# Row sums of a windowed attention block: half of them from exponentials with an accumulator on ScalarE

## The reference

```
q, k, v = xn Wq' + bq, xn Wk' + bk, xn Wv' + bv      16 heads of 32
scores  = q k' / sqrt(32), masked where (i % 256) < (j % 256)
probs   = softmax(scores);  attn = probs v
s       = attn Wo' + bo
y       = clip((xn sign(Wf)') * scale + bias, -100, 100)
out     = x + s * y * sigmoid(y)
```

## Time and profile before

| | us |
|---|---|
| median of three runs | 1762.6 |
| profiled execution, device time | 1763.97 |
| its span, first to last instruction | 1762.2 |
| PE busy | 1701.8 |
| DVE busy | 1385.3 |
| POOL busy | 1295.9 |
| ACT busy | 972.8 |

### The profile page before, as it was taken

One profiled execution on the slowest core, in us unless ns is written; L12 is line 12 of the kernel. 1 busy time (PEld: TensorE's weight loads), 2 busy tenths in 40 slices (PEclk: granted clock), 3 DMA queues, 4 the chain that ended last, 5 costly groups with the idle time before them and its releaser, 6 DMA issues.

```text
span 1762.2 us, 33805 instructions
## 1 busy us (share of the span) xinstructions
PE 1701.8 (97%) x11996; PEld 792.9 (45%) x11996; DVE 1385.3 (79%) x2392; ACT 972.8 (55%) x1765; POOL 1295.9 (74%) x1280
## 2 busy tenths in 40 slices
PE   7998999999999999999999999999999999999888
PEld 3443444444444444444444444444444444444333
DVE  6888778797788877798778977778778797688862
ACT  4366655565555655556555566546665565555553
POOL 0087677886878778887788867798777886877883
PEclk9999999999999999999999999999999999999999
DMA  7313311242123412233122431224312232122111
GB/s 207 107 38 85 77 40 55 79 103 73 40 60 90 115 39 54 66 98 85 43 67 61 106 78 32 77 67 102 69 43 59 79 93 59 31 63 72 43 49 49
DMA packets 161273, 125.52 MB, mean 71 GB/s; under 512 B 83152, under 2 KB 135504, under 8 KB 160656
## 3 DMA queue, kind: packets, MB, share of 16 engines
q1 hardware_dynamic: 160144, 122.58, 26.6%
q10 hardware_dynamic: 960, 0.79, 0.2%
HBM read 41.23 MB, written 16.78 MB: 33 GB/s over the span
## 4 chain that ended last, share of the span: by engine, by line
PE 77%; DVE 9%; POOL 6%; issue 4%; ACT 3%; ACTq 0%; DMA 0%; SPq 0%; POOLq 0%; DVEq 0%
PE pJ L453 28%; PE pO L656 13%; PE pS L612 9%; PE pT L636 9%; POOL acc L1087 3%; PE pJ L545 3%; PE pJ L549 3%; PE pJ L546 3%; DVE mx L963 3%; PE pT L632 3%; PE pS L615 3%; PE pT L596 3%; DVE HL L934 2%; ACT PT L776 1%; ACT xs L693 1%
## 5 line engine op out<-in xcount | busy, mean ns | idle before, releaser
L1087 POOL TENSOR_TENSOR acc<-acc,PT 128x384 f32<-128x384 f32 (+1 forms) x744 | 884.2, 1222 | 280.1 <-PE pO L656 280.1
L963 DVE TENSOR_REDUCE mx<-pS 128x1 f32<-128x512 f32 (+3 forms) x1216 | 768.0, 649 | 193.1 <-PE pS L615 128.4
L776 ACT ACTIVATE PT<-pT 128x512 f32<-128x512 f32 (+1 forms) x960 | 537.0, 567 | 551.8 <-PE pT L636 496.1
L612 PE MATMUL pS<-QK 96*128 96x512 f16 (+3 forms) x1280 | 393.5, 318 | 20.9 <-DVE mx L963 19.9
L636 PE MATMUL pT<-QK 97*128 97x512 f16 (+3 forms) x1280 | 391.7, 317 | 6.4 <-DVE R L1006 3.9
L656 PE MATMUL pO<-PT,V 128*32 128x512 f32 (+3 forms) x2560 | 234.2, 473 | 0.2 <-ACT PT L776 0.2
L612 PEld LDWEIGHTS pS<-QK 96*128 96x128 f16 x1280 | 124.2, 97 | 195.4 <-DVE mx L963 58.5
L776 ACT ACTIVATE acc<-pT 128x512 f32<-128x512 f32 x256 | 151.4, 596 | 84.4 <-PE pT L636 82.0
L453 PE MATMUL pJ<-xT,wh_q 128*128 128x512 f16 x512 | 193.4, 380 | 1.9 <-ACT xT L711 1.5
L453 PE MATMUL pJ<-wh_v,xT 128*128 128x512 f16 x512 | 192.7, 379 | 1.6 <-DVE sg L952 1.6
L453 PE MATMUL pJ<-xT,wh_k 128*128 128x512 f16 x512 | 192.9, 378 | 0.0
(11 more groups left out here) (151 smaller groups left out, 2229.2 us busy)
## 6 DMA issues: line engine op xcount, KB each, us to landing
QK<-sg SPq DMA_DIRECT2D x756, 64.0 KB
xs<-in_x SPq DMA_DIRECT2D x60, 256.0 KB, 3.1
xr<-in_x SPq DMA_DIRECT2D x58, 256.0 KB, 3.0
out<-xr SPq DMA_DIRECT2D x58, 256.0 KB, 2.5
QK<-aT SPq DMA_DIRECT2D x256, 1.0 KB, 1.7
QK<-in_x SPq DMA_DIRECT2D x8, 256.0 KB, 3.7
QK<-in_mqk SPq DMA_DIRECT2D x2, 512.0 KB, 8.9
PT<-in_wvT SPq DMA_DIRECT2D x1, 1024.0 KB, 12.0
```

Source lines behind the costliest of these rows:

```text
L612: ins = e.matmul(s_bank("s", i)[:, base:base + wide], q4[0:96, j, qc], k4[0:96, j, 0:wide], start=True, stop=True)
L776: e.activation(to, t_bank("t", i)[:, 0:cols], ACT.Exp, scale=SS).then_inc(s_p, 1)
L963: e.tensor_reduce(mx[:, par, part, :].rearrange("p (j q) -> p j q", q=4)[:, heads[0]:heads[-1] + 1, qi], s_bank("s", i)[:, 0:cols].rearran ...
L1087: e.tensor_tensor(a, a, PT[:, RING_AT[i] % NPT, 0:width * len(heads)].rearrange("p (j q) -> p j q", j=len(heads)), ALU.add).then_inc(s_ap, 1)
```

## The change

For the 32 even units and for unit 63 (`ROW`, 33 units) the row sums come from the S chunks: once DVE has a chunk's maxima, it scales them at once to that chunk's shifts (`row_shifts`, L1023 of the new kernel), and ACT takes the exponential of the scores in place in PSUM, one instruction per head and query block, with the shift as its bias and a sum over the row written by the accumulator output (`sum_rows`, L808). A pS bank of such a chunk is free only after ACT has done so. For unit 63, whose rows lie in two chunks with two different maxima, the two partial sums are rescaled by exp of the differences and added. The 16 sums per row block are then moved by SP through a scratch in HBM into the layout that the reciprocals need (`move_sums`: one DMA, then four that wait for it). The even units have no additions on POOL and DVE any more, no product with ones and no first transpose; unit 63 has no products with ones, and unit 62 neither. The 31 odd units up to 61 are summed as before, with one acc instead of two. The ring has twelve rooms, and key block 0 of the even units goes through it too. For unit 63 DVE multiplies pO by the reciprocals directly and in two halves, and DVE instead of POOL makes the low halves.

The S chunks of an even unit are planned 1.4 units of time apart, those of an odd unit 0.82 apart, and nearly all other planned times change a little.

```diff
-NPT = 9
+NPT = 12
...
+                CHUNKS.append((38 * (_n // 2 - 1) + ((3 + 1.4 * _k) if _n % 2 == 0 else (18.3 + 0.82 * _k)),
+                               (_n, _qi, _part, _w, range(_j, _j + _heads))))
...
+ROW = [n for n in range(NU) if n % NQS == 0 or n == NU - 1]
...
 def at_sums(n):
-    return (at_pv(n + 1, 1) if n not in SUMMED else at_pv(n, 4 * (n % NQS) + 3)) + 0.01
+    return at_pv(n + 1, 1) + 0.01 if n not in ROW_AT else at_pv(n, 4 * (n % NQS) + 3) - -1.17
...
-        return SL * (a - 2) + ((3.97, 13.7, 17.61, 18.35), ...
+        return SL * (a - 2) + ((4.3, 15.37, 17.61, 18.51), ...
...
-        acc = sb("acc", [P, 2, 4, 512], F32)
+        acc = sb("acc", [P, 4, 512], F32)
...
+            if old == "s" and j in CHUNK_AT:
+                return s_e, CHUNK_AT[j] + 1
...
             def row_sums():
-                for n in range(NU - 2):
+                for n in range(NU):
+                    if n in ROW_AT:
+                        continue
...
-                        if n in SUMMED:
-                            if kb == 0:
-                                ln.wait_ge(*s_bank_free("sm", n))
-                            for j in range(4):
...
-                                ins = e.matmul(sums_bank(n)[32 * j:32 * j + 32, 512 - width:512], ones[:, :], probs,
-                                               start=kb == 0, stop=kb == nkb - 1)
...
+            def sum_rows():
+                for i in ROW_CHUNKS:
+                    n, qi, part, width, heads = S_TILES[i]
+                    yield at_s(i) + 1.81
+                    if ROW_AT[n] >= 2:
+                        ln.wait_ge(s_rq[ROW_AT[n] % 2], 64 * (ROW_AT[n] // 2))
+                    ln.wait_ge(s_ac, CHUNK_AT[i] + 1)
+                    for k, j in enumerate(heads):
+                        c = 4 * j + qi
+                        scores = s_bank("s", i)[:, k * width:k * width + width]
+                        ins = e.activation(scores, scores, ACT.Exp, bias=row_shift(i)[:, c:c + 1], scale=SS,
+                                           accum_out=rS[:, ROW_AT[n] % 2, part, c:c + 1])
+                    ins.then_inc(s_e, 1)
...
+            def row_shifts():
+                for i in ROW_CHUNKS:
...
+                    yield at_s(i) + 0.16 + 0.43
...
+                    ln.wait_ge(s_a, i + 1)
+                    of = (slice(None), slice(heads[0], heads[-1] + 1), qi)
+                    e.tensor_scalar(row_shift(i).rearrange("p (j q) -> p j q", q=4)[of],
+                                    mx[:, n % 2, part, :].rearrange("p (j q) -> p j q", q=4)[of], -SS, None,
+                                    ALU.mult).then_inc(s_ac, 1)
...
             def normalise():
...
+                    if n in ROW_AT:
+                        ln.wait_ge(s_rq[ROW_AT[n] % 2], 64 * (ROW_AT[n] // 2 + 1))
+                        e.reciprocal(rc[:, :], rq[:, ROW_AT[n] % 2].rearrange("p i q -> p q i")).then_inc(s_rc, 1)
...
+            def last_outputs():
+                for h in range(2):
...
+                    e.tensor_tensor(On[1][:, cs], pO[:, cs], R[:, cs], ALU.mult).then_inc(s_on, 1)
+                for h in range(2):
...
+                    e.tensor_tensor(last_half(Onl, h), On[1][:, 256 * h:256 * h + 256], last_half(Onh, h),
+                                    ALU.subtract).then_inc(s_ol, 1)
...
+            def move_sums():
...
+                    ln.wait_ge(s_e, chunks(n))
...
+                    e.dma_start(moved[par], rS[:, par, 0, :]).then_inc(s_rd[par], 16)
...
+                    ln.wait_ge(s_rd[par], 16 * (ROW_AT[n] // 2 + 1))
+                    for j in range(4):
+                        e.dma_start(rq[32 * j:32 * j + 32, par, :, :],
+                                    moved[par].rearrange("(i b) (j q) -> j b i q", b=32, j=4)[j]).then_inc(s_rq[par], 16)
```

More of the change, by code:

```diff
@@ L100, in at_s @@
 def at_s(i):
[L101 to L102 removed]
+    return CHUNKS[i][0]
 def at_t(i):
@@ L398, in gate, with last_half, row_shift, probabilities_at @@
             return xs[:, k, :] if 0 <= k < 4 else xr[k - 4][:, :] if k in (4, 5) else U[i % 2][:, :]
-        def sums_bank(n):
-            return s_bank("sm", n) if n in SUMMED else t_bank("sm", n)
+        def last_half(to, h):
+            return to[:, (GN - 1) % NSLOT, 512 + 256 * h:768 + 256 * h]
+        def row_shift(i):
+            n, _, part, _, _ = S_TILES[i]
+            return ap[:, part, :] if n == NU - 1 else a16[:, n % 2, 0:16]
+        def probabilities_at(i):
+            n, kb, width, heads = T_TILES[i]
+            if kb == 0 and n not in ROW_AT:
+                return acc[:, heads[0], :]
+            return PT[:, RING_AT[i] % NPT, 0:width * len(heads)]
         def bank(kind, a, b=0):
@@ L775, in probabilities @@
[L775 to L776 removed]
+                    if i not in RING_AT:
+                        ln.wait_ge(s_sm, n // 2)
+                    elif RING_AT[i] >= NPT:
+                        i0 = RING[RING_AT[i] - NPT]
+                        n0, kb0, _, _ = T_TILES[i0]
+                        ln.wait_ge(s_pv, units(n0) + kb0 + 1)
+                        if i0 in ADD_P_AT:
+                            ln.wait_ge(s_ap, ADD_P_AT[i0] + 1)
+                        elif i0 in ADD_V_AT:
+                            ln.wait_ge(s_av, ADD_V_AT[i0] + 1)
@@ L1038, in last_results @@
                     e.tensor_tensor(result(i), gate(i), rest(i), ALU.add).then_inc(s_fv, 1)
-            in_time(maxima(), shifts(), additions(), normalise(), constants(), split_weights(), output_bias(),
-                    first_layer_norm(), layer_norm(), split_x(), take_xt(), stage_qk(), gates(), results(), last_results())
+            in_time(maxima(), row_shifts(), shifts(), additions(), normalise(), constants(), split_weights(), output_bias(),
+                    first_layer_norm(), layer_norm(), split_x(), take_xt(), stage_qk(), gates(), last_outputs(), results(), last_results())
         @block.gpsimd
@@ L1090, in normalise @@
             def normalise():
-                for n in range(NU):
+                for n in range(NU - 1):
                     gn, qs = divmod(n, NQS)
                     s, cs = gn % NSLOT, slice(qs * 512, qs * 512 + 512)
-                    yield past("sm", n) + 1.01
+                    yield past("sm", n) + (0.32 if n in ROW_AT else 0.98)
                     ln.wait_ge(s_R, n + 1)
```

251 lines of the change are left out of this document (144 added, 107 removed).

## The result

The new kernel takes 1749.51 us (median of four runs, 1748.9 to 1751.11) against 1762.4 on the same chip: ratio 0.9929, interval 0.9912 to 0.9946. It is faster, by 12.9 us where 28.6 were forecast. A second measurement of it, later and beside its own runs of the kernel before (1762.99), gave 1749.88 and 0.9920 (0.9907 to 0.9934). The time is inside the range and almost exactly that of the accumulator case (1750), in part by luck, as shown further down. The profiled execution has a span of 1748.0, 14.2 less than before.

The account below looks back on a forecast made before the run. PE was taken to bound a batch; from a span of 1762.2 us, -26.7 - 7.7 - 0.5 + 7 + 3 + 5 - 5 - 4 = -28.9, plus 1.8 minus 1.4, gave 1734 us; range 1717 to 1757.

Parts of the forecast that it names:

- accumulator case: Rival, chance 0.20: each accumulator sum costs ACT 0.14 us extra, layer norm stretches cost 23 us instead of 7; 1750 us.
- PE's terms: On PE, 31 removed sums of even units save 26.7 us; removed products with ones of units 62 and 63 save 7.7.
- the end: After the last product with V, PE's other matmuls cover the shorter chain, so it gains only about 0.5 us.
- ring: Twelve rooms and faster additions mostly remove ACT's waits for POOL in the middle: 5 us gained (0 to 8).
- POOL: Near the end, where POOL is busy while PE idles, lighter POOL work gains 4 us (0 to 8).
- the forecast's own sign of being wrong: Forecast is wrong if PE's waits for pS and pT together exceed 60 us, or PE's work did not fall some 34.
- Score exponentials on ACT: On ACT, even units' exponentials (512 columns: 686 ns) add 6.5 us per unit; layer norm stretches overrun 1.1 us, seven batches.
- The accumulator: On ACT, writing the accumulator costs near nothing (upper bound 4.5 us per even unit); ACT's term 7 us, 0 to 39.
- Chain through DVE: In even units, late DVE scalings hold ACT's exponentials and make PE wait: 0.1 us per unit, 3 us in all.
- slower rival: Rival, chance 0.11: late DVE scalings hold T exponentials 2.2 us per even unit, 70 us; 1798 or more, as pauses lower clock.
- Unit 63: In the 30 us from 1660, 27 scalings and 32 exponentials fill DVE and ACT: 5 us lost (0 to 12).
- case of more gained: Rival, chance 0.15: half of PE's 27 us behind the maxima goes, ACT and unit 63 cost nothing; 1719 us.

Follow-up runs that it names:

- e2: New kernel with a single one-column exponential per score chunk in place of all its exponentials and sums: 1716.74 us, ratio 0.9731 to the kernel before.
- e1: New kernel with its score exponentials but without their accumulator output, sums taken from a constant: 1732.05 us, ratio 0.9816 to the kernel before.
- e10: New kernel with each scaling of a score chunk's maxima planned 0.01 instead of 0.43 units of time after the maxima: 1753.88 us, ratio 0.9933.
- e3: New kernel with unit 63 summed as before by products with ones, all else unchanged: 1745.38 us, ratio 0.9889 to the kernel before.
- e5: New kernel with nine rooms for probabilities instead of twelve: 1760.40 us, ratio 0.9973 to the kernel before.
- second trace: The new kernel run once more, unchanged, on the chip of the later experiments: 1749.88 us, ratio 0.9920 to the kernel before.
- e9: New kernel with unit 63 summed by products with ones and the second halves' f16 copies of x on POOL: 1737.09 us, ratio 0.9847.
- e4: New kernel with one more one-column ACTIVATE ahead of each of the 544 exponentials, nothing left out: 1806.70 us, ratio 1.0238 to the kernel before.

## Why the prediction was right or wrong

- **What bounds the kernel** (PE, and a matmul removed in the middle is worth its length): right. With most of ACT's new load gone (e2) 46.5 us of span come off; PE's terms, the end, ring and POOL were -26.7 - 7.7 - 0.5 - 5 - 4 = -43.9. The page of e2 shows the two halves: PE is busy for 33.8 us less than before, the forecast's 34, and idle for 12.7 less.

```profile
PE 1668.0 (97%) x11652; PEld 781.1 (46%) x11652; DVE 1319.9 (77%) x2621; ACT 1026.0 (60%) x2145; POOL 1158.1 (68%) x1154
```

  In the new kernel PE's busy time fell by only 19.6 us, so the forecast's own sign of being wrong, that PE's work did not fall by some 34 us, is there on the page. The matmuls are gone as planned; the other 14.2 us are time that PE takes longer over the same matmuls than in e2, where only ACT's load differs. Some 5 us of them are the clock, by my estimate from 0.992 of 1748.0 us granted against 0.995 of 1715.7; the rest no run separates.
- **Score exponentials on ACT**: right. By start-to-start times the forecast's 686 less 120 ns is 0.57 us for 512 columns, and 0.57 was measured; 581 less 120 is 0.46, and 0.46 was measured. For all that was budgeted against the gain (7 + 3 + 5 = 15 us) the exponentials without reads cost at least 13.5 (e1 against e2): 6 in the middle, where 7 + 3 were forecast, 5.3 at unit 63 and 2.3 at the start, which the sum left out.
- **The accumulator**: this is the step that failed. "What writing the accumulator costs, no row shows ... I take a value near nothing, because the accumulator belongs to an instruction that passes over the data anyway". It is an instruction of its own, 0.1 us of the stream, and the 544 of them cost 18.8 us (e1), more than the 14.7 by which the forecast missed; the other terms erred by 4 the other way. The formula would have borne it in part: with 0.1 us each the excess is 1.1 + 16 x 0.1 = 2.7 us, seven times, 19 us for the term in place of 7, so 11 us for the reads. They cost 11.9 in the middle, but only some 60% of what a batch lost lies in the layer norm group, where the formula put all, and 6.6 us lie at the start and at unit 63, outside it. The reason given was an argument about what the instruction does, not a row; the Trainium skill's rule for VectorE (VectorE: DVE Perf Modes, section on two Vector instructions with no wait between them), weighed beside it, pointed the other way.
- **The accumulator case** had the right mechanism: 0.14 us each, batch 211, 1750; measured 0.10, 210.3, 1749.5. That the time came out to half a microsecond is luck. With the 0.10 that was measured its own sum gives about 1746. It priced the reads too high, left out the 6.6 us that they cost at the start and at unit 63, and the other errors of the forecast made up the rest.
- **Chain through DVE, 3 us**: not measured. ACT waits 8.0 us for the scalings, and planning them earlier gained nothing (e10), but it made PE wait for DVE elsewhere. The slower rival, 70 us, falls all the same. Its second half, that a PE that pauses loses clock as well, is seen where ACT makes PE pause: 0.77 to 0.81 in the stretch of unit 63. The Trainium skill (TensorE: Matmul & The Clock Gate, HAM oscillation) describes a kernel whose clock falls again at each of its repeated waits. Its waits are for DMA and longer; the trace agrees that repeated waits bring the lower level, here with pauses of at most 1.5 us each.
- **Unit 63, 5 us (0 to 12)**: its sums cost 10.7 us in their stretch (e3), near the upper bound. Reads are 4.6 of that, by the fall from the new kernel to e1; the exponentials' own part is 5.3 (e1 to e2). So 5 was the right size without reads. Much of it is clock: from e2 to the new kernel the stretch grows by 9.8 us, and PE's busy time for almost the same matmuls by 6.5. Set against what the products and the end give back (7.9), the unit should have been left alone; the forecast, at 5 against 5.5 + 0.5, saw no loss.
- **Ring**: nine rooms cost 8.9 us of span (e5), the forecast's 5 (0 to 8) was for the step from before, where key block 0 did not go through the ring. The two are not the same quantity, so the term itself stays unmeasured.
- **PE's waits behind the maxima**, 27.1 us, were at nothing in the sum, and only the case of more gained took half of them off. In the new kernel they are 4.5 and in e2 4.8, so this half of the case came true, and more. The gain is in e2's 12.7 us of idle time; in the new kernel ACT's load takes it back. Which of the new spacing of the chunks, the ring and the lighter POOL does it, no run separates. That case's price was also added up wrong: half of 27 us with ACT's 7 and unit 63's 5 is 25.5 us and 1708, not 15 and 1719.
- **The start**, up to unit 1, was not in the sum. It is 0.4 us longer than before, which is not clear of noise, and 4.4 longer than in e2 (3.2 in the second trace); up to 2.0 of that are reads.
- **The end**: no pause of PE above 0.5 us for the last chain, as forecast. From the sums of unit 61 to the end 6.1 us are gone, where the forecast had 7.7 for the products and 0.5 for the end; where the other 2 are, no run shows.

What stays open: how e2's 12.7 us less idle time divide between ring, POOL and the spacing of the chunks (the forecast had 5 + 4 for ring and POOL, and 2.2 of the 12.7 are the one long pause of before), and what the chain through DVE costs.

## What to carry to other kernels

When an engine's average is 55% but one of its stretches is at 80%, price what you add to it from one start to the next in a full stretch, and count every instruction that one line issues: 544 reads of 0.1 us cost 18.8 of the 34.9 us that the change took from PE. If no row shows an operation, take the price that bears on the decision and not the comfortable end of the bounds. Before work is moved off the full engine, look at the receiving engine in the very stretch: half of the copies moved to POOL gained 7 us, and moving the other half as well, into a group where POOL was denser, made the kernel 39 us slower than e9.

## What the runs showed of the hardware

- An ACTIVATE with an accumulator output is followed on ScalarE by ACTIVATION_READ_ACCUMULATOR. It is shown with 253 ns in the mean and takes 0.09 to 0.10 us from a full stream.
- The accumulator output doesn't lengthen the exponential itself: 0.57 us for 512 columns and 0.46 for 384, start to start, with it and without it (e1).
- An ACTIVATE of one column takes 0.18 to 0.19 us from a full stream when it reads SBUF (e4) and 0.14 us in place in PSUM (e2), both with a bias from SBUF. A read of the accumulator is cheaper than either.
- Exponentials in place in PSUM with a bias from SBUF take 0.57 us for 512 columns, start to start, against 0.48 for those from PSUM to SBUF without a bias.
- Scalings of one column on DVE are shown with 149 ns, where the one of 16 columns before had 282.
- PE busy for 45.6 of 57.6 us in short pieces, with pauses of at most 1.5 us each, was granted 0.77 to 0.81 of the clock; busy for 39.1 of 47.8 us (e2, where PE's work is almost the same) 0.93.
